# Attention values in three rounded products for all batches; one query tile's 5x5 convolution on TensorE by 2x2 phases, the other on VectorE and GpSimd

## The reference, cut to what matters

```
# layer 0: linear attention over qkv and over a convolved copy of it
qkv = [x@wq, x@wk, x@wv]                       # 768 channels, 32 heads of 8
dw  = depthwise 5x5 conv(qkv, dw_kernel)       # SAME
pw  = grouped 1x1 conv(dw, pw_kernel)          # groups of 8
for each head of [qkv, pw]:                    # 64 heads, n = 1024 positions
    q, k = relu(q), relu(k); v = [v, 1]
    scores = v @ k.T ; out = scores @ q ; out = out[:8] / (out[8] + 1e-15)
y  = batchnorm(proj 1x1 (out)) ; x1 = y + x
# layer 1: softmax attention over the 1024 positions, 256 channels
norm = (x1 - mean) / sqrt(var + 1e-5)          # per channel
attention = softmax((f_w norm + f_b).T @ (g_w norm + g_b))   # 1024 x 1024
out = o_w (h_w x1 + h_b) attention.T + o_b + x1
```

## Time and profile before

| what | value |
|---|---|
| median of three runs | 652.06 us (652.04 to 652.4) |
| the profiled execution | 653.32 us, its span 651.5 us |
| granted TensorE clock, mean | 0.995 of full speed |
| busy PE / DVE / ACT / POOL | 612.1 / 524.2 / 472.8 / 494.0 us |
| DMA, mean | 26 GB/s |

### The profile page before, as it was taken

How to read it: one execution, slowest core, us unless ns; L and a number is a source line. 1 busy time by engine, 2 the same in 40 slices (tenths; PEclk the granted TensorE clock), 3 DMA queues, 4 the chain that set the end, 5 groups by cost and what they waited for, 6 DMA issues and landing times.

```text
span 651.5 us, 13132 instructions
## 1 busy us (share of the span) xinstructions
PE 612.1 (94%) x5448; PEld 442.6 (68%) x5448; DVE 524.2 (80%) x616; ACT 472.8 (73%) x772; POOL 494.0 (76%) x236
## 2 busy tenths in 40 slices
PE   4997999989899999999899999999899999899997
PEld 3864366646678887556578886556568875376897
DVE  4899899777899799977899999969889995274543
ACT  4697679888686798988687897997688685244331
POOL 4859949967999999959999999989999996013000
PEclk9999899999999999999999999999999999999999
DMA  8000000101100000001200000000100000000000
GB/s 319 3 10 5 1 3 3 65 2 64 65 2 17 16 18 19 1 2 64 66 1 17 16 18 18 3 1 1 64 1 18 16 19 18 0 1 1 16 17 33
DMA packets 6698, 16.67 MB, mean 26 GB/s; under 512 B 880, under 2 KB 1136, under 8 KB 6128
## 3 DMA queue, kind: packets, MB, share of 16 engines
q1 hardware_dynamic: 6640, 15.84, 6.8%
HBM read 11.64 MB, written 4.19 MB: 24 GB/s over the span
## 4 chain that ended last, share of the span: by engine, by line
PE 80%; DVE 8%; ACT 6%; POOL 2%; issue 2%; DMA 1%; SPq 0%; POOLq 0%; DVEq 0%; ACTq 0%
PE ps L762 14%; PE ps L786 13%; PE ps L878 7%; PE ps L597 4%; PE ps L531 4%; PE ps L777 4%; PE ps L535 4%; PE ps L532 4%; PE ps L810 3%; PE ps L844 2%; DVE ps L1371 2%; PE ps L635 2%; ACT prod L1071 2%; PE ps L697 2%; PE ps L580 2%
## 5 line engine op out<-in xcount | busy, mean ns | idle before, releaser
L1639 POOL TENSOR_TENSOR conv<-conv,prod 128x930 f32<-128x930 f32 (+4 forms) x174 | 381.8, 2236 | 35.0 <-ACT prod L1071 32.0
L1371 DVE SCALAR_TENSOR_TENSOR ps<-raw,dw_sb,ps 128x930 f32<-128x930 f32 (+4 forms) x264 | 317.3, 1202 | 6.8
L1071 ACT ACTIVATE prod<-raw,dw_sb 128x961 f32<-128x961 f32 (+4 forms) x209 | 217.8, 1109 | 5.3 <-POOL conv L1639 3.9
L786 PE MATMUL ps<-ht,pt 128*128 128x256 f32 x384 | 87.4, 381 | 0.0
L786 PEld LDWEIGHTS ps<-ht,pt 128*128 128x128 f32 x384 | 71.1, 190 | 11.5 <-issue 2.5
L1239 ACT ACTIVATE rows<-ps,small 128x1024 f32<-128x1024 f32 x32 | 35.6, 1114 | 58.7 <-DVE small L1560 58.4
L1639 POOL TENSOR_TENSOR rows<-rows,prod 128x930 f32<-128x930 f32 (+4 forms) x26 | 58.2, 2239 | 11.7 <-ACT prod L1071 8.1
L1555 DVE TENSOR_REDUCE small<-ps 128x1 f32<-128x1024 f32 x32 | 39.1, 1222 | 20.5 <-PE ps L762 20.5
L762 PE MATMUL ps<-hi,t_hi 128*128 128x512 f32 x128 | 43.9, 424 | 8.1 <-DVE t_lo L1543 5.3
L762 PE MATMUL ps<-lo,t_hi 128*128 128x512 f32 x128 | 39.9, 392 | 0.0
L531 PE MATMUL ps<-hi,wqkv_hi 128*128 128x512 f32 x92 | 37.8, 411 | 0.0
(11 more groups left out here) (185 smaller groups left out, 1168.3 us busy)
## 6 DMA issues: line engine op xcount, KB each, us to landing
q_raw<-x_dram SPq DMA_DIRECT2D x8, 512.0 KB, 5.6
x<-x_dram SPq DMA_DIRECT2D x4, 1024.0 KB, 4.7
out_dram<-x_t SPq DMA_DIRECT2D x16, 256.0 KB, 2.0
conv<-wqkv_dram SPq DMA_DIRECT2D x1, 768.0 KB, 4.2
conv<-fg_dram SPq DMA_DIRECT2D x1, 512.0 KB, 6.1
proj_sb<-proj_dram SPq DMA_DIRECT2D x1, 512.0 KB, 7.7
pw_sb<-pw_dram SPq DMA_DIRECT2D x1, 384.0 KB, 6.9
mask_sb<-masks_dram SPq DMA_DIRECT2D x1, 280.0 KB, 6.2
```

The lines of the kernel that those rows point to most:

```text
L786: mm = pe.matmul(dst[:, 0:C], pt[:, i % PT_BUFS, j, :], ht[:, j, :], start=(j == 0), stop=(j == NB - 1))
L1071: act.activation(dst, view, ACT.Copy, scale=weight(t, i)).then_inc(prod_ready, 1)
L1371: return dve.scalar_tensor_tensor(dst, view, w, before, ALU.mult, ALU.add)
L1639: pool.tensor_tensor(total, total, product, ALU.add).then_inc(conv_pool, 1)
```

## The change

- `values` is the three-product form for every batch. Its operands need room: `pt_hi` takes the place of `pt`, `pt_lo` that of `x1`, `ht_hi` that of `kt` and `vt`, `ht_lo` overwrites `ht`. The load of the next batch's residual into `x1` therefore moves in SP's order behind the last `values`. ACT gets four casts of `ht` per batch, DVE 16 subtractions, POOL four (`ht_lows`, at the third entry of `RSTD_AT`).
- Query tile 0 is convolved on PE for all taps and batches. ACT writes its raw values not as an image but as four phase images (even and odd rows and columns, 18x18 with borders) into `stage`; SP moves them with 16 DMAs of 32 partitions from SBUF to SBUF (`load_phases`) so that each group of 32 partitions holds 8 channels in four phases; `phase_conv` then needs 9 offsets of 16 matmuls (32x32, 256 columns) with tap weights (`taps_phases`) that SP loads anew for each batch, since they lie where `t_hi` and `t_lo` are. ACT evicts four half banks (`phase_sums`). It stands in the middle stage of the batch ahead, after the second `output_weights`. `queries` of tile 0 is eight matmuls of 128x32 by 256 columns per half.
- Query tile 1 has no PE taps: 7 (batch 0: 9) are ACT's and POOL's late taps, 18 (16) are DVE's. All `quads` but those of tile 5 in batch 0 go, and with them their sums and joining products.
- DVE's taps: 68 (batch 0: 66). POOL's adds per later batch: 48 and 6 late ones. All tables are new; of them `TAPS_HT` has nine taps before the fold of body 0.

```diff
-LATE_OF = (9, 10, 10, 10)
-SHARED_OF = (0, 3, 3, 3)
-QUAD_OF = (16, 12, 12, 12)
+LATE_OF = (9, 7, 7, 7)
+SHARED_OF = (0, 0, 0, 0)
+PHASE_TILE = 0
+OFFSETS = [(ey, ex) for ey in (-1, 0, 1) for ex in (-1, 0, 1)]
...
-TAPS_HT = ((1, 0, 1, 0), (0, 0, 0, 0), (1, 1, 1, 1))
-TAPS_MAX = ((0, 2, 0, 4, 2, 0, 2, 5, 1, 8), (0, 1, 3, 4, 2, 5, 3, 6, 0, 0), (0, 0, 4, 4, 4, 2, 4, 6, 2, 1))
+TAPS_HT = ((0, 9, 0, 1), (0, 1, 0, 0), (3, 0, 1, 1))
+TAPS_MAX = ((0, 0, 0, 2, 3, 3, 2, 2, 1, 8), (0, 1, 0, 3, 3, 1, 2, 1, 1, 1), (1, 0, 1, 3, 2, 2, 2, 1, 2, 10))
-FIRST_SPLIT = 9
+FIRST_SPLIT = 24
...
+            def load_phases(b):
+                sp.wait_ge(a_free, A_RQ[b][2 * PHASE_TILE + 1] + 1)
+                for f in range(PHASES):
+                    for g in range(QUADS):
+                        sp.dma_start(phased[f::PHASES, g, :], stage[g::QUADS, f, :]).then_inc(phases_loaded, 16)
...
+            def phase_conv(b):
+                pe.wait_ge(taps_loaded, 16 * (b + 1))
+                pe.wait_ge(phases_loaded, 16 * PHASES * QUADS * (b + 1))
+                for e, (ey, ex) in enumerate(OFFSETS):
+                    for r in range(QUADS):
+                        k = slice(r * QUAD, (r + 1) * QUAD)
+                        bank = a_slot(A_AT["sums", b] + r) if e == 0 else a_bank(A_AT["sums", b] + r)
+                        for g in range(QUADS):
+                            view = phased_img[k, g, 1 + ey:PSIDE - 1 + ey, 1 + ex:PSIDE - 1 + ex]
+                            mm = pe.matmul(bank[g * QUAD:(g + 1) * QUAD, 0:QUARTER], tap_weights[k, e, g, :], view,
+                                           start=(e == 0), stop=(e == len(OFFSETS) - 1))
+                mm.then_inc(a_full, QUADS)
...
             def values(b, i):
                 pe.wait_ge(t_free, 16 * b + 2 * (i + 1))
+                if i == 0:
+                    pe.wait_ge(ht_lo_ready, D_HT * (b + 1))
...
+                    high, low = pt_hi[:, i % PT_BUFS, j, :], pt_lo[:, i % PT_BUFS, j, :]
+                    pe.matmul(dst[:, 0:C], high, ht_hi[:, j, :], start=(j == 0), stop=False)
+                    pe.matmul(dst[:, 0:C], high, ht_lo[:, j, :], start=False, stop=False)
+                    mm = pe.matmul(dst[:, 0:C], low, ht_hi[:, j, :], start=False, stop=(j == NB - 1))
...
+                if t == PHASE_TILE:
+                    for x in range(2):
+                        for r in range(QUADS):
+                            mm = pe.matmul(dst[r * QUAD:(r + 1) * QUAD, x * QUARTER:(x + 1) * QUARTER],
+                                           pw_ph[:, r, 2 * h + x, :], conv_ph[:, r, :], start=True, stop=True)
...
                 pe.wait_ge(t_free, 16 * (b + 1))
-                if with_next:
-                    pe.wait_ge(exp_done, NB * (b + 1))
-                    shared_quads(b + 1, 0)
-                (values if with_next else last_values)(b, NB - 1)
+                values(b, NB - 1)
...
-                    if 1 <= i <= NB and not with_next:
+                    if 1 <= i <= NB:
                         for u in range(2):
-                            dve.wait_ge(last_pt_hi_ready, 2 * (i - 1) + u + 1)
+                            dve.wait_ge(pt_hi_ready, 16 * b + 2 * (i - 1) + u + 1)
```

More of the change, by code:

```diff
@@ L64 @@
 Q_TILES = (0, 1)
[L67 removed]
+QUAD_UNITS = [(5, 0), (5, 1)]
 FIRST_TILE = 5
@@ L200, in conv_seq_kernel @@
         t_lo = sb("t_lo", [P, CK, N], F32R)
[L201 to L206, removed]
+        phased = nc.alloc_sbuf_tensor_at("phased", [P, QUADS, PIMG], F32, offset=sums_at)
+        tap_weights = nc.alloc_sbuf_tensor_at("tap_weights", [P, len(OFFSETS), QUADS, QUAD], F32,
+                                              offset=sums_at + 4 * QUADS * PIMG)
+        raw = sb("raw", [P, TILES - 1, IMG])
+        stage = sb("stage", [P, PHASES, PIMG])
         conv = sb("conv", [P, TILES, N])
@@ L843, in body @@
                         if t < 2 * CK:
-                            pe.matmul(dst[:, c0:c0 + P], block, pw_sb[:, t, :], start=True, stop=True)
+                            pe.matmul(dst[:, c0:c0 + P], block, pw_sb[:, 2 * CK + t - 1, :], start=True, stop=True)
                         else:
@@ L1102, in sums, with phase_sums @@
                     act.copy(quad_sums[h][:, r, :], a_bank(slot + r)).then_inc(a_free, 1)
+            def phase_sums(b):
+                slot = A_AT["sums", b]
+                act.wait_ge(a_full, slot + QUADS)
+                for r in range(QUADS):
+                    act.copy(conv_ph[:, r, :], a_bank(slot + r)[:, 0:QUARTER]).then_inc(a_free, 1)
             def first_sums(n):
@@ L1387, in conv_taps @@
                     before = None if starts else acc
-                    if t == SHARED_TILE and starts and SHARED_OF[b]:
-                        before = final
-                        dve.wait_ge(conv_pool, add_count(b, len(ADD_SEQ[b])))
                     tap(final if i == NTAPS - 1 else acc, t, i, before).then_inc(conv_dve, 1)
@@ L1714 @@
     pw_bd[:, 2 * CK:] = pw_bd[:, 2 * CK:].transpose(2, 1, 0).copy()
-    pw_quads = np.stack([pw_bd[r:r + QUAD, :CK, r:r + QUAD] for r in range(0, P, QUAD)], 2)
-    pw_quads = np.tile(pw_quads, (QUADS, 1, 1, 1)).reshape(P, CK, P)
+    group, unit, ch = np.meshgrid(np.arange(QUADS), np.arange(QUADS), np.arange(D), indexing="ij")
+    channel = QUAD * unit + QUADS * ch + group
+    pw_phases = np.zeros((P, QUADS, PHASES, QUAD), pw.dtype)
+    taps_phases = np.zeros((P, len(OFFSETS), QUADS, QUAD), dw.dtype)
+    for t in (PHASE_TILE,):
+        for f in range(PHASES):
+            for co in range(QUAD):
+                pw_phases[QUAD * group + D * f + ch, unit, f, co] = pw_bd[channel, t, QUAD * unit + co]
+            for to in range(PHASES):
+                for e, (ey, ex) in enumerate(OFFSETS):
+                    dy, dx = 2 * ey + f // 2 - to // 2 + PAD, 2 * ex + f % 2 - to % 2 + PAD
+                    if 0 <= dy < TAPS and 0 <= dx < TAPS:
+                        taps_phases[QUAD * unit + PHASES * ch + f, e, group, D * to + ch] = dw[t * P + channel, TAPS * dy + dx]
     head_rows = np.tile(np.kron(np.eye(HEADS), np.ones((1, D))), (QUARTERS, 1))
```

286 lines of the change are left out of this document (140 added, 146 removed).

## The result

The changed kernel takes 643.25 us (median of four runs, 641.08 to 646.07) against 652.23 us of four runs of the kernel before: ratio 0.984, interval 0.981 to 0.987. It is faster by 9.0 us, where 20.4 were forecast; 643.25 lies in the stated range. The profiled execution is its fastest run: 641.08 us, span 639.2, 12.3 us less than the span before. The distance from 12.3 to 9.0 is that this run lies 2.2 us under its median and the profiled run before 1.1 over the 652.23; of the four runs, the slower ones show the lower mean granted clock, 0.971 in the slowest against 0.979 in the fastest.

The account below looks back on a forecast made before the run. PE (94% busy) was taken to bound the kernel only narrowly, with POOL and DVE close behind. -14.2 - 21.8 - 5.4 + 14.7 - 6.7 + 4.5 + 1.5 + 4 + 3 = -20.4 gave 631.7 us median, range 617 to 646.

Parts of the forecast that it names:

- Values: Attention blocks of batches 0 to 2: 24 rounded products take 2.87 us instead of 3.46, -14.2 us in all.
- The last queries of batch 0: Start of the kernel: PE's last tile 1 queries end near 111.7 instead of 118.4, -6.7 us.
- The quads and queries in the fronts: From `pwkv` to queries, three later batches: dropped quads and cheaper queries, less a wait at `scores`, -15.7 us.
- The wait behind the convolution: Middle stage: transposes wait for ACT to evict the convolution's first slot, about 0.58 us (0.4 to 1.5).
- the last rival: Phases come late: 16 transfers run one after another and PE waits before its convolution; 684 us at 3 us each; chance 0.06.
- step (c): Middle stage of body 0: nine DVE taps before the fold outlast PE's work, +4 us (0 to 5).
- the phase convolution: Middle stage: nine offsets of 16 matmuls take 4.3 us; with the wait 4.9 a batch, +14.7 in three.
- DVE becomes the bound: Full cycles: DVE keeps its 17 us of idle, cycle 150.4, total about 654 us; chance 0.13.
- (d): Two full cycles: POOL, and DVE with 9 us of idle, 1 to 2 us late, +3 us (0 to 10).
- POOL and DVE over 92% busy in a cycle: Sign of a right forecast: in a cycle both engines are busy over 92% of the time.
- cycles of 142 to 144: Sign of a right forecast: a cycle takes 142 to 144 us, against 147.7 before.

Follow-up runs that it names:

- e1: Changed kernel with one of nine offsets in the phase convolution, all batches: 650.73 us, ratio 0.995 to the kernel before.
- e7: Changed kernel with the two inner loops of the phase convolution exchanged: 645.31 us, ratio 0.989 to the kernel before.
- e4: Changed kernel with about half the columns (128 in the rows) in every phase-convolution matmul: 644.54 us, ratio 0.986 to the kernel before.
- e2: Changed kernel with the 29 DVE taps ahead of the fold working on one image row of 32: 636.99 us, ratio 0.975 to the kernel before.
- e11: e6's order on PE and ACT with the changed kernel's tap tables: 655.60 us, ratio 1.006 to the kernel before.
- e12: e6's tap tables with the changed kernel's order on PE and ACT: 666.77 us, ratio 1.022 to the kernel before.
- e5: Changed kernel with the fold ahead of PE's convolution and most stage taps, convolution cut in two around the third output weights: 635.98 us, ratio 0.975.
- e6: e5 with the convolution in one piece, third and fourth output weights behind it: 636.32 us, ratio 0.976 to the kernel before.
- e9: e5 with one DVE tap a batch moved to where DVE idles between its output-weight additions: 632.28 us, ratio 0.968 to the kernel before.
- e10: e9 with one tap of batch 2 moved from the projection into the attention: 631.98 us, ratio 0.969 to the kernel before.

## Why the prediction was right in sign and short by half

*Right.* Values of 2.83, forecast 2.87. The last queries of batch 0 end at 112.4, forecast 111.7. The quads and queries in the fronts, -14.6 of -15.7. The wait behind the convolution, 0.55 to 0.66, forecast 0.58. And the last rival falls: the 16 phase transfers of batch 2 go out in one row of SP's queue, their issues done at 276.95, their last packet ends at 278.41, and PE starts the convolution of that batch at 296.62 without a wait.

```profile
266.35 10.60 SPq L487 DMA_DIRECT2D phased<-stage  x16
```

The rule of the Trainium skill that the prediction weighed there ("DMA: Bandwidth & Descriptors", section "Anatomy of one DMA — SWDGE (gpsimd) path", about 2.0 us for every DMA on that path) would make 32 us of these 16 one after the other; the trace does not show them that way: they take 12.1 us from the first issue to the last packet.

*Wrong: step (c).* It read "In body 0 nine taps, 10.8 us, stand before DVE's fold" and priced +4, in batch 0 alone. (Its 2.2 us up to the end of the spread are 2.4 in the earlier trace rows, which is of no weight here.) The tables put ten there in body 1 (six behind the projection, three in `TAPS_STAT`, one in `TAPS_HT`) and ten in body 2, in other rows than the one the step had looked at. The fold's low part moved from 10.4 to between 19.4 and 19.9 us after the projection in all three batches, and e1 shows that it stays there with most of PE's convolution gone. From there to the first energy both kernels need about 9.0: 28.3 to 28.9 in all, against a forecast of 24.3 (28.3 in batch 0). That is 4 us in each of two more batches, 8 of the 10 missed. The rest is 0.5 in batch 0 and the clock in batch 2, where the fourth output weights behind a wait of 2.5 us took 3.60 instead of 1.97. In batches 0 and 1 the clock fell under the third output weights, ahead of the wait for the fold, and e7 shows for batch 0 that this cost nothing. That 643.25 still lies in the range is due to the range's width: the bounds given to step (c), 0 to 5, do not hold the about 12 us (4 in each of three batches) that it cost.

*Mis-sized beside it: the phase convolution*, 4.3 forecast and 6.3 to 6.8 measured. The reason given was columns, from the earlier trace rows; e4 shows that columns alone don't set it. By luck this error cost next to nothing in the result, since the taps' lane covered it: with PE's lane alone (e2) a stage of batch 1 takes 26.8, with the taps 28.3. Had the tables been right, it would have been the larger error, 2.6 us a batch (26.8 in place of 24.3).

On this the Trainium skill ("TensorE: Matmul & The Clock Gate", section "Part 3: Packing small matmuls — row/col tiling") has a rule: tiles packed into the array take one matmul's time and about 4 ns for each further tile. An estimate from it, with 0.40 for one (the records' median is 396 ns), is 0.52 us for the 32 records of an offset and 4.7 for nine. The trace does not agree: 263 records in 5.36 us are 20 ns each.

*Named among the rivals, in part.* "DVE becomes the bound" was the rival that came closest, with the wrong place: it expected lateness in the attentions, where sixteen subtractions were added; these became shorter by all that was forecast, and DVE bound in the middle stage, where its taps had been gathered. Of (d), 3 us in the two full cycles, 2.5 can be seen: their stretches from the queries to the end of the projection are 1.0 and 1.4 longer. Of this only 0.83, in batch 2, is a new wait of PE for DVE. The +0.3 in the list of spans above is what is left of it, because the same stretch of batch 0 became 2.1 shorter, where the kernel before waits 2.12 for issue alone. Two signs named for a right forecast failed: "POOL and DVE over 92% busy in a cycle" (88 to 91%) and cycles of 142 to 144 (146.1 and 145.2).

## What to carry to other kernels

Where two engines work side by side toward one join, price both lanes up to that join, in every batch, and take the later one; filler work in an in-order queue counts by where it stands, and all the tables that feed the stretch have to be read. Taking work off the shorter lane gains nothing (e1), and can lose when the engine that now waits is slowed by its clock. Moving the join ahead of both lanes and the filler behind it gained, by the ratios, 6 us over the changed kernel (10 with DVE's order mended), where each half of that move alone lost 14 and 25.

## What the runs showed that was not expected

- The length of a stream of 32x32 float32 matmuls with fresh weights for each hardly followed its columns: 6.4 us for 288 records of 256 columns and 6.2 for as many of 128 (batch 2). What the fewer columns gave was lost in pauses of up to 1.8 us, each of which ended 1.20 to 1.55 us after a packet of instructions.
- Idle time of PE can be paid twice. The granted clock fell in all three middle stages of e1, e11 and e12, where PE waited up to 8.4, 5.8 and 7.3 us at a time, and in none of the twelve of e5, e6, e9 and e10. What decides in between stays open: it fell in all three stages of the changed kernel, in two of e7 and in only one of e2, whose stage of batch 1 has the same convolution (6.70 us against 6.39) and waits as short (0.65 for issue and 0.66 behind it, against 0.33 and 0.66).
